# Layer 1's expert outputs mixed inside the rounds of layer 2's attention, and layer 0's feed-forward written out turn by turn

## What is computed

```python
x = x + L0_xattn(layernorm(x), ctx);  x = x + L0_ffn(layernorm(x))
x = x + L1_xattn(layernorm(x), ctx);  x = x + L1_ffn(layernorm(x))
x = x + L2_xattn(layernorm(x), ctx);  x = x + L2_ffn(layernorm(x))
x = x + L3_xattn(layernorm(x), ctx);  x = x + L3_ffn(layernorm(x))

def L1_ffn(x):                      # x here is the normalised input
    idx, w = top_2(x @ Wg + bg); w = softmax(w)
    eo = [relu(x @ W1[e] + b1[e]) @ W2[e] + b2[e] for e in idx]
    y = w[0] * eo[0] + w[1] * eo[1] + x
    return gamma * (y - mean(y)) / sqrt(var(y) + 1e-5) + beta

def L2_xattn(q, c):                 # 16 heads of 64
    p = softmax((q @ Wq) @ (c @ Wk).T / 8)
    return (p @ (c @ Wv)) @ Wo

def L0_ffn(x):                      # 8 heads of 32, 16 experts, the best two by gate
    t = heads(x @ Wm + bm); g = top_2_of(softmax(t @ emb))
    return sum_e(g[e] * (gelu(t @ W1[e] + b1[e]) @ W2[e] + b2[e])) @ Wo + bo
```

## Time and profile before

| | us |
|---|---|
| median of 3 runs | 3848.06 |
| lowest and highest run | 3845.46, 3849.7 |
| profiled execution | 3863.81 |
| its span, first to last instruction | 3862.0 |

### The profile page before, as it was taken

How to read it: one execution, slowest core, us unless ns; L and a number is a source line. 1 busy time by engine, 2 the same in 40 slices (tenths; PEclk the granted TensorE clock), 3 DMA queues, 4 the chain that set the end, 5 groups by cost and what they waited for, 6 DMA issues and landing times. The chain is left out here.

```text
span 3862.0 us, 77246 instructions
## 1 busy us (share of the span) xinstructions
PE 2987.0 (77%) x24429; PEld 2127.0 (55%) x24438; DVE 2346.0 (61%) x5118; ACT 1646.6 (43%) x2756; POOL 1205.2 (31%) x1311
## 2 busy tenths in 40 slices
PE   5996999999889960799049999995655799823980
PEld 4884222222268850799038888884333577623970
DVE  5887565655345562344665555556998798852652
ACT  3774888989534420233013333332444466500110
POOL 1111555655324415300511221111000677433005
PEclk9997999999989985899569999998777899966995
DMA  2001444435230042222210000000000433322223
GB/s 96 15 15 48 122 123 118 128 112 133 81 126 15 15 149 75 65 71 70 83 59 8 5 7 5 7 7 15 1 0 0 183 110 114 113 81 86 91 90 120
DMA packets 179724, 266.53 MB, mean 69 GB/s; under 512 B 22528, under 2 KB 129152, under 8 KB 173440
## 3 DMA queue, kind: packets, MB, share of 16 engines
q1 hardware_dynamic: 167152, 230.74, 19.1%
q0 software_dynamic: 12432, 34.10, 2.8%
HBM read 194.49 MB, written 61.87 MB: 66 GB/s over the span
## 5 line engine op out<-in xcount | busy, mean ns | idle before, releaser
L2182 ACT ACTIVATE params<-L0f_Z,params 128x1024 f32<-128x1024 f32 x512 | 533.0, 1113 | 95.5 <-PE L0f_Z L2239 95.3
L2158 POOL TENSOR_TENSOR L0f_mixed<-L0f_mixed,L0f_gated 128x512 f32<-128x512 f32 x240 | 323.0, 1346 | 307.3 <-DVE L0f_gated L2404 305.9
L2239 PE MATMUL L0f_Z<-params,L0f_w_stacked 128*128 128x512 f16 x1024 | 299.3, 391 | 41.1 <-ACT params L2182 23.2
L2404 DVE SCALAR_TENSOR_TENSOR L0f_gated<-L0f_O,params 128x512 f32<-128x512 f32 x240 | 180.0, 750 | 224.1 <-PE L0f_O L2248 198.9
L833 POOL TENSOR_TENSOR L2x_probs<-L2x_probs,L2x_recip_den 128x512 f32<-128x512 f32 x128 | 132.1, 1043 | 585.1 <-DVE L2x_recip_den L1040 585.1
L2248 PE MATMUL L0f_O<-params 128*32 128x512 f32 x2048 | 277.0, 613 | 0.5 <-ACT params L2182 0.5
L2239 PEld LDWEIGHTS L0f_Z<-params,L0f_w_stacked 128*128 128x128 f16 x1024 | 71.1, 99 | 298.0 <-ACT params L2182 258.2
L1868 ACT ACTIVATE L1ftiles_hidden<-L1ftiles_H,L1ftiles_b_tile 128x128 f32<-128x128 f32 x292 | 83.4, 369 | 305.8 <-PE L1ftiles_H L1891 305.8
L1038 DVE TENSOR_REDUCE L2x_recip_den<-L2x_probs 128x4 f32<-128x512 f32 x128 | 86.9, 679 | 199.8 <-ACT L2x_probs L857 199.8
L857 ACT ACTIVATE L2x_probs<-L2x_probs 128x512 f32<-128x512 f32 x128 | 80.3, 628 | 206.3 <-DVE L2x_probs L1032 206.3
L1987 POOL DMA_INDIRECT L1fcombine_gathered<-rows_out_dram,L1f_slots x64 | 61.6, 963 | 291.3 <-PEq L1969 258.7
(11 more groups left out here) (508 smaller groups left out, 7559.7 us busy)
## 6 DMA issues: line engine op xcount, KB each, us to landing
params<-gates_dram SPq DMA_DIRECT2D x512, 128.0 KB, 3.1
params<-side_dram SPq DMA_DIRECT2D x32, 1024.0 KB, 5.0
rows_in_dram<-L1froute_zero SPq DMA_DIRECT2D x2, 4864.0 KB, 23.5
L1ftiles_rows<-rows_in_dram SPq DMA_DIRECT2D x76, 128.0 KB, 2.0
rows_in_dram<-L3froute_zero SPq DMA_DIRECT2D x2, 4864.0 KB, 22.9
L3ftiles_rows<-rows_in_dram SPq DMA_DIRECT2D x76, 128.0 KB, 2.0
rows_out_dram<-L1ftiles_outputs SPq DMA_DIRECT2D x72, 128.0 KB, 1.7
rows_out_dram<-L3ftiles_outputs SPq DMA_DIRECT2D x72, 128.0 KB, 1.7
```

Of the source, the lines that this page charges most:

```text
L2158: pool.tensor_tensor(acc[:, b.slot, m % KT, :], acc[:, b.slot, m % KT, :], tmp[:, m % 2, :], ALU.add).then_inc(mixed, 1)
L2182: act.activation(hid[:, n % 4, :, :], Z[:, n % 2, :, :], ACT.Gelu, bias=w["b1"][:, n // 4:n // 4 + 1]).then_inc(hid_ready, 1)
L2239: mm = pe.matmul(Z[:, n % 2, s, :], w1s[:, e, :], stack[:, b.slot, t, 2 * half + s, :], start=True, stop=True)
L2404: dve.scalar_tensor_tensor(out=out, in0=O[:, m % 2, :], scalar=w["b2"][:, e:e + 1], in1=gb[:, e % AHEAD, m % KT, :], op0=ALU.add, op1=ALU. ...
```

## The change

Two edits that don't depend on each other.

1. `combine` isn't run for layer 1. Its gathers and its arithmetic go into layer 2's attention, two tiles at a time: `add_experts` (weigh and add both outputs, statistics) stands in even rounds behind `center` 2, and `small_steps` for its root behind `center` 3; `close_experts` (apply the norm, add to x, statistics of the new x for the attention's own norm) and its root stand at the same places in odd rounds. The pair that is mixed in round r holds tiles r + 4 and r + 5, and is closed a round later, just ahead of its first `norm_row`. The statistics of all 32 tiles ahead of the phase go. POOL issues four gathers before its first division, and then two behind the second and two behind the fourth division of every odd round, each pair of tiles behind a wait for the mixing of the pair before. `kept`, `slot`, `share` live until the attention ends (a scope of their own, closed there); to make room, qT, kT, v, p and oT move to unused columns of a parameter store. The loop covers rounds 1 to 26; POOL's list is written out.
2. In `head_experts_phase` the six middle turns are written out on all five engines.

```diff
@@ -754,7 +754,7 @@
     dh, NT, BT, UH, NG = 64, 8, 4, 4, 4
     w, c = sh.params(phase), sh.const
-    FIRST, LAST = 1, BATCH - 3
+    FIRST, LAST = 1, BATCH - 5
...
@@ -783,28 +783,33 @@
     with ExitStack() as ctx:
         core = Core(nc, ctx, phase)
-        norm = Norm(core, BATCH)
+        mixed_norm, norm = Norm(core, 2, "close"), Norm(core, 2)
+        both = core.sb("gathered", [P, 2, 2, D])
+        acc = core.sb("mixed", [P, 2, D])
+        shares = core.sb("shares_now", [P, 2, 2])
         xn = core.sb("xn", [P, D])
         xnT = core.sb("xnT", [P, KT, P])
         cT = core.sb("ctxT", [P, 2, KT, P])
-        qT = core.sb("qT", [P, 2, NT, P])
-        kT = core.sb("kT", [P, 2, NT, P])
-        v = core.sb("values", [P, 2, HEADS * dh])
-        p = core.sb("probs", [P, NG, UH, P])
+        n = NT * P
+        qT, kT = (sh.scratch(next_phase, k * 2 * n, (2, n)).rearrange("p s (t q) -> p s t q", t=NT) for k in range(2))
+        v = sh.scratch(next_phase, 4 * n, (2, n))
+        p = sh.scratch(next_phase, 6 * n, (NG, UH, P))
         pT = core.sb("probsT", [P, NG, UH, P])
         mx = core.sb("row_max", [P, NG, UH])
         rc = core.sb("recip_den", [P, NG, UH])
-        oT = core.sb("heads_outT", [P, NT, P])
+        oT = sh.scratch(next_phase, 8 * n, (NT, P))
...
         ctx_loaded = [core.sem(f"ctx{s}_loaded") for s in range(2)]
-        (xn_ready, scored, centered, exped, divided, turned, turned_out, summed, normed, norm_step, max_step, sum_step, recip_step) = (
+        gathered, mix_step = core.sem("experts_gathered"), core.sem("mix_step")
+        (xn_ready, scored, centered, exped, divided, turned, turned_out, summed, normed, max_step, sum_step, recip_step) = (
             core.sem(s) for s in (
                 "xn_ready", "scored", "centered", "exped", "probs_divided", "probs_turned", "probsT_ready", "heads_summed",
-                "heads_out", "norm_step", "max_step", "row_sums", "recip_step"))
+                "heads_out", "max_step", "row_sums", "recip_step"))
+        MIXED, CLOSED, SHIFTED, PER = 5, 5 + RSQRT_STEPS, 9 + RSQRT_STEPS, 9 + 2 * RSQRT_STEPS
         block = ctx.enter_context(nc.Block())
         @block.sync
...
@@ -828,17 +833,29 @@
         @block.gpsimd
         def _(pool):
+            def gather(b):
+
+                if b.round:
+                    pool.wait_ge(mix_step, (b.round - 1) * PER + 3)
+                for k in range(2):
+                    pool.indirect_dma_start(out=both[:, b.slot, k, :], out_offset=None, in_=sh.dram["rows_out"],
+                                            in_offset=bass.IndirectOffsetOnAxis(ap=mixture.slot[:, k, b.n:b.n + 1], axis=0)
+                                            ).then_inc(gathered, 16)
+
             def divide(b, g):
                 pool.wait_ge(recip_step, b.n * NG + g + 1)
                 pool.tensor_tensor(p[:, g, :, :], p[:, g, :, :], rc[:, g, :].unsqueeze(2).broadcast_to([P, UH, P]),
                                    ALU.mult).then_inc(divided, 1)
-            def work(r):
-                if holds(r, 1):
-                    for g in range(NG):
-                        divide(r.plus(1), g)
-
-            rounds(pool, work)
+            for k in range(2):
+                gather(Turn(0, k))
+            for r in range(-3, BATCH + 1):
+                b = Turn(0, r)
+                for g in range(NG):
+                    if holds(b, 1):
+                        divide(b.plus(1), g)
+                    if r % 2 and g % 2 and holds(b, 5 + g // 2):
+                        gather(b.plus(5 + g // 2))
         @block.scalar
         def _(act):
...
@@ -1002,8 +1019,55 @@
         @block.vector
         def _(dve):
+            def linked(b, done):
+                return Steps(dve, mix_step, b.round * PER + done)
+
+            def small_steps(norm, steps):
+                rsqrt(dve, steps, norm.mean_var[:, :, 1], norm.half[:, :], norm.root[:, :], norm.tmp[:, :], LN_EPS)
+
+            def add_experts(b):
+
+                steps = linked(b, 0)
+                steps.link(dve.tensor_copy(shares[:, :, :], mixture.share[:, :, bass.ts(b.round, 2)]))
+                dve.wait_ge(gathered, (b.round + 1) * 64)
+                for k in range(2):
+                    for j in range(2):
+                        last = dve.scalar_tensor_tensor(out=acc[:, j, :], in0=both[:, j, k, :], scalar=shares[:, k, j:j + 1],
+                                                        in1=acc[:, j, :] if k else mixture.kept[:, b.n + j, :], op0=ALU.mult, op1=ALU.add)
+                    steps.link(last)
+                mixed_norm.moments(dve, steps, lambda j: acc[:, j, :])
+
+            def close_experts(b):
+
+                steps = linked(b, CLOSED)
+                for j in range(2):
+                    last = dve.scalar_tensor_tensor(out=acc[:, j, :], in0=acc[:, j, :], scalar=mixed_norm.mean_var[:, j, 0:1],
+                                                    in1=mixture.gamma, op0=ALU.subtract, op1=ALU.mult)
+                steps.link(last)
+                for j in range(2):
+                    row = sh.x[:, b.n + j, :]
+                    last = dve.scalar_tensor_tensor(out=row, in0=acc[:, j, :], scalar=mixed_norm.root[:, j:j + 1], in1=row,
+                                                    op0=ALU.mult, op1=ALU.add)
+                steps.link(last)
+                detach_wait(dve)
+                norm.moments(dve, steps, lambda j: sh.x[:, b.n + j, :])
+
+            def pair_sums(r):
+
+                if r.slot == 0 and holds(r, 4):
+                    add_experts(r.plus(4))
+                if r.slot == 1 and holds(r, 3):
+                    close_experts(r.plus(3))
+
+            def pair_roots(r):
+
+                if r.slot == 0 and holds(r, 4):
+                    small_steps(mixed_norm, linked(r.plus(4), MIXED))
+                if r.slot == 1 and holds(r, 3):
+                    small_steps(norm, linked(r.plus(3), SHIFTED))
+
             def norm_row(b):
-                at = bass.ds(b.n, 1)
+                at = slice(b.slot, b.slot + 1)
                 if later(b):
                     dve.wait_ge(banks.filled("xT"), banks.until_filled("xT", b.plus(-1)))
                 dve.tensor_scalar(xn[:, :], sh.x[:, b.n, :], norm.mean_var[:, at, 0], norm.root[:, at],
...
@@ -1052,8 +1116,12 @@
                     invert_sums(nxt, 0)
                     invert_sums(nxt, 1)
                     center(nxt, 2)
+                pair_sums(r)
+                if ahead:
                     invert_sums(nxt, 2)
                     center(nxt, 3)
+                pair_roots(r)
+                if ahead:
                     invert_sums(nxt, 3)
                 if holds(r, 3):
...
@@ -1067,11 +1135,8 @@
             sh.wait_params(dve, phase)
             banks.open(dve)
-            steps = Steps(dve, norm_step, 0)
-            for j in range(BATCH):
-                last = dve.bn_stats(norm.stats[:, j, :], sh.x[:, j, :])
-            steps.link(last)
-            norm.finish(dve, steps)
+            pair_sums(Turn(0, -4))
+            pair_roots(Turn(0, -4))
             rounds(dve, work)
             dve.wait_ge(banks.emptied("proj"), banks.until_emptied("proj", Turn(0, BATCH - 1)))
...
@@ -1577,12 +1649,13 @@
     w, c = sh.params(phase), sh.const
     rows_in, rows_out = sh.dram["rows_in"], sh.dram["rows_out"]
     with ExitStack() as ctx:
+        lasting = Core(nc, outer if relu else ctx, phase)
+        kept = lasting.sb("normalized", [P, BATCH, D])
+        slot = lasting.sb("slots", [P, 2, BATCH], I32)
+        share = lasting.sb("shares", [P, 2, BATCH])
         core = Core(nc, ctx, phase)
-        kept = core.sb("normalized", [P, BATCH, D])
         gate = core.sb("gates", [P, BATCH, E])
         lg = core.sb("logits", [P, BATCH, E])
-        slot = core.sb("slots", [P, 2, BATCH], I32)
-        share = core.sb("shares", [P, 2, BATCH])
         expert = core.sb("tile_experts", [P, TILES + TILES_AHEAD], I32)
         route(nc, sh, phase, w, c, kept, lg, rows_in, next_phase)
...
@@ -1602,7 +1675,9 @@
                     pool.wait_ge(scattered, 2 * BATCH * 16)
         compute_tiles(nc, sh, phase, w, c, expert, rows_in, rows_out, relu, NF)
-        combine(nc, sh, phase, w, slot, share, kept, rows_out, relu)
+        if not relu:
+            combine(nc, sh, phase, slot, share, rows_out)
+    return Mixture(kept, slot, share, w) if relu else None
 def route(nc, sh, phase, w, c, kept, lg, rows_in, next_phase):
...
@@ -2001,23 +2075,12 @@
                     for k in range(2):
                         for j in range(G):
-                            base = acc[:, j, :] if k else kept[:, t * G + j, :] if relu else row(j)
-                            out = row(j) if k and not relu else acc[:, j, :]
+                            base = acc[:, j, :] if k else row(j)
+                            out = row(j) if k else acc[:, j, :]
```

(22 more changed lines are left out.)

32 lines of the change are left out of this document (15 added, 17 removed).

## The result

| | median, us | lowest to highest, runs | time against before, 95% interval |
|---|---|---|---|
| before | 3848.88 | 3845.46 to 3851.77, 4 | |
| after | 3730.74 | 3729.01 to 3732.4, 4 | 0.9697 [0.9685, 0.9709] |

The change takes off 118.1 us, some 3%. The prediction was 3725.1 us with a range of 3714 to 3750, so the time lies within the range and 5.6 us above the point. The profiled execution of after took 3729.6 us (span 3727.8), close to its median, while that of before was 15 us above its own. That difference matters further down.

A forecast was written before the change was run, and what follows sets the result against it. VectorE was taken to bound layer 1's combine stage, TensorE the attention behind it. Savings of 113.2 + 11.55 - 1.8 = 122.95 us off the 3848.06 us median gave 3725.1 us, range 3714 to 3750.

The forecast's parts named there:

- Layer 0 without a loop: Layer 0's feed-forward: straight code removes the cost of two backward branches, 11.55 us saved, bounds 0 and 11.55.
- The rival by which straight code brings nothing: Layer 0's feed-forward: the stall comes from fetching and straight code pays it too; 3737 us, chance 0.06.
- The combine stage: Start of layer 2's attention: first normalised row at 1867.4 instead of 1980.61 us, 113.2 us saved.
- The load beside the gathers: Start of layer 2's attention: gathers beside the next parameter load land 2 us later, bounds 0 and 6.5.
- the gathers wait for the parameter load: Rival, start of layer 2's attention: first gathers wait for the whole load, 4.5 us more, 3730 us, chance 0.05.
- The opening scope: Before layer 2's attention: one more scope is closed before the phase starts, costing 0.9 us.
- The rounds: Layer 2's attention rounds: 171 us of added VectorE work fits idle gaps, cost 0, bounds 0 and 1 us a round.
- the rounds give part of it back: Rival, layer 2's attention: 0.5 to 1.0 us over 30 rounds, 3740 to 3755 us; chance 0.17 with loop stalls.
- Room: Layer 2's attention rounds: a late VectorE costs nothing up to about 0.07 + 0.81 + 0.94 = 1.8 us per round.
- slower: Rival, layer 2's attention: VectorE's chain becomes the round's length, all 171 us exposed, 3896 us, chance 0.04.
- The closing scopes: Ends of layer 2's attention and layer 3's feed-forward: one more scope closing each, 0.9 us apiece, 1.8 us in the sum.
- part 2: The old combine stage's removal ahead of layer 2's attention: 113.2 us saved up to the first normalised row.

The follow-up runs named there:

- straight_only: The kernel before with only layer 0's feed-forward written out turn by turn on all five engines; 3833.5 us, 0.9966 of before.
- the second profile: The kernel before, unchanged, profiled once more; its one time is 3848.05 us, its span 3846.2 us.
- load_later: The changed kernel, with SyncE issuing layer 2's next parameter load only after the first eight gathers have landed; 3721.81 us, 0.9681 of before.
- before_again: The kernel before, unchanged, run again beside the follow-up kernels; profiled span 3846.2 us, first to last normalised row 638.4 us.
- ahead_of_sums: The changed kernel with both parts of the mixing moved ahead of the two inversions and the centering they stood behind; 3873.15 us, 1.0067 of before.

## Why the prediction was right, and where its sizes were off

**Layer 0 without a loop: right.** Term 11.55 us; the first and the last of the exponential's table loads that bound the four turns are 11.54 us closer (501.53 to 815.02 against 503.16 to 828.19), and `straight_only` was timed 10.5 us below before. The rival by which straight code brings nothing falls. Beyond the forecast, the split by engines shows that TensorE's branch carries most of the cost and that writing out the other four alone saves nothing that can be told from zero, 1.06 us with an interval that reaches it; they are worth 2.1 us once TensorE's is gone. One reading was off without a consequence: the prediction has ScalarE's GELU set the pace, but in a turn of before (503 to 581 us) TensorE is busy for 75.6 of 78 us and ScalarE for 69.5.

**The combine stage: right in its mechanism, 12 us off in its size.** From the last output tile to the first normalised row it went from 129.2 us in the second profile to 27.8, a saving of 101.4 us where the term had 113.2. Three parts account for the 11.8 us.
- *The base was one execution's, 8.6 us.* The prediction subtracted a stage measured in a profiled execution 15.75 us above the median, and took the whole of that stage off the median. It had noted the 15.75 us, but did not ask where they lay. The trace held most of the answer: one turn of 19.5 us among turns of about 12.
- *The load beside the gathers, 5.7 us instead of 2, so 3.7 more.* This is nearly the rival "the gathers wait for the parameter load", with a chance of 0.05, whose bound was 6.5; the wait is that long because both share the DMA engines, and not because the gathers stand behind the whole load. `load_later` shows it, since with the load held back VectorE starts 5.74 us sooner behind the gathers. The reason given for the low end, 0.5 MB against 3.9 MB on another queue, is no protection.
- *The opening scope, 0.3 us where the term had 0.9, so 0.6 the other way.* From SyncE's last output store to POOL's first gather it is 3.42 us before and 3.75 after. 8.6 + 3.7 - 0.6 = 11.7 of the 11.8 us.
- The chain of two rows was 10.99 us for 11.0.

**The rounds: right.** They hold the 171 us of VectorE's work for 0.5 us (639.3 against 638.8; against `before_again` 0.9), where the term had 0 and the rival "the rounds give part of it back" 15 to 30. VectorE's idle time before the third sums is 0.55 us (forecast near 0.4), before the fourth 0.28 (near 0). Room was 2.65 us rather than 1.8, mostly since the normalised row (line 1009 before, 1073 after) takes 0.38 us in after, where it took 1.1 in the loop before. The diff holds a likely cause that the prediction passed over: in the loop before, this instruction took its mean and root at a column given by the round (`bass.ds(b.n, 1)`), and now at a fixed one (`slice(b.slot, b.slot + 1)`). The four such rows of before that stand ahead of the loop, with constants, took 0.38 to 0.41 us as well, and the first in the loop 1.08. No run changed this alone. POOL's gathers stay at 940 to 1252 ns, median 989, beside VectorE's work, against 943 to 1206, median 949, in the old stage. The Trainium skill (SBUF — State Buffer, SBUF: two separate sides) has POOL unable to write a gather's descriptors while VectorE holds the port pair that they share. No such lockout shows in this mix of instructions: the first four gathers, issued while VectorE stood idle, took 940 to 980 ns each, and the median beside its work is at most some 5% above that. That the work's place decides, and not its amount, is what `ahead_of_sums` shows: the rival "slower" was the right mechanism for another order of the same instructions, at 144.5 us of the 171, part of it the clock's.

**The closing scopes: 1.8 us in the sum, mostly not spent.** The step from the last normalised row to layer 2's feed-forward is 74.5 us in both traces (2494.4 to 2568.9, 2619.4 to 2693.9). From the last mixing instruction of layer 3 to the end of the span it is 18.3 us against 17.6.

**The sum.** By the profiles it is 11.5 + 101.4 - 0.9 = 112.0 us; the timed saving is 118.1 in the first comparison and 115.5 in the second. The spans of `before_again` and after differ by 118.4: 12.6 up to the last output tile of layer 1, 101.4 in the stage, -0.9 in the rounds, and 5.3 spread over what follows, most of it in small pieces of layer 3's routing, whose code is the same. From the last normalised row of layer 3's attention to its first expert output that part took 222.2 to 225.9 us in five profiles of kernels with the old stage, 221.1 to 224.6 in seven with the new one (221.1 or 221.2 in four). Whether the change brings these few us or the executions scatter, no run settles. It is also why the prediction ended only 5.6 us off. Of its saving of 122.95 us the spans lack 122.95 - 118.4 = 4.55 us, which is 11.8 too much in part 2 and 0.9 for the rounds, less the 5.3 us behind the rounds, the 1.8 us of scopes (whatever they did cost is within the 5.3) and 1.1 more than its term ahead of the stage. The mechanisms were forecast; that the point came so close was in good part luck, since errors of some 13 and 8 us lay in opposite directions.

**A version that beats both.** `load_later` is the changed kernel with one wait more, at 3721.81 us.

## What to carry to other kernels

Before a stage's length is taken off a median, compare its like turns with one another or take a second profile: a turn of 19.5 us among turns of 12 is no part of what a change can save. Work moved into another stage's idle time is free in the gap that it fills, and may cost more than the gap elsewhere: follow the releases from the place where it is put to the bound engine, and count how many us lie between. When a new first step waits for a small transfer, look at what large load is issued in the same microsecond, and let that load wait.

## What was not expected of the hardware

- Four gathers of 0.5 MB in all, issued within 4 us of a load of 3.9 MB on another queue, took 7.66 us instead of 1.92 from the last one's end on POOL to the instruction that waited for them; one of them took 8.5 us to land, where 3.7 is the longest without the load.
- TensorE's gaps of some 3.3 us in each round took the mean granted clock from 1.00 to 0.93, and so cost some 1.5 us a round above their own length, though seven of 28 gaps were followed by matmuls at full clock.
- In layer 0's loop a backward branch costs TensorE 3.3 to 3.9 us of "issue", and VectorE stands idle for 3.5 to 3.9 us at its own, 2.3 to 2.6 us more than at a turn without one. In the attention's loop, with the mixing in its rounds, neither engine has one: TensorE is busy for all of the 500 us from 2000 on, and no wait of VectorE's there is for "issue". The Trainium skill (Runtime: NRT & Kernel Launch, Instruction fetch mechanics) has a branch stall only where its target is no longer resident; a stall in the one loop and none in the other agrees with that, though no run here measured what was resident.
